# Layer norm and routing by block in the stages ahead of the experts of a six-layer network, experts on blocks 0 to 2 first, attention written out

## The reference

```python
x = x + 0.5 * ffn(ln(x))        # stage 0: silu(w1 x) * (w2 x), gelu, gelu, w3; 512 hidden
x = x + mixer(ln(x))            # stage 1: selective scan
x = x + 0.5 * ffn(ln(x))        # stage 2
x = x + 0.5 * moe(ln(x))        # stage 3
x = x + attention(ln(x))        # stage 4: 8 heads of 128, causal, k and v shared
x = x + 0.5 * moe(ln(x))        # stage 5

def _route(x, gate_w, gate_bias):
    scores = jax.nn.sigmoid(x @ gate_w.T)                       # 64 experts
    choice = scores + gate_bias
    group_scores = sum of the top 2 of each of 8 groups         # choice, 8 experts a group
    masked = where(group in the top 4, choice, 0)
    w = scores at the top 8 of masked
    return 2.5 * w / sum(w), zero elsewhere
# moe: sum over 64 experts (88 hidden) of rw[t, e] * silu(x Wg) * (x Wu) @ Wd, plus a shared one of 176
```

## Time and profile before

| What | us |
|---|---|
| Median of 3 runs (lowest, highest) | 1802.55 (1801.62, 1803.52) |
| Profiled execution | 1803.61 |
| Its span in the trace | 1801.8 |
| Start of stage 3 to the first weighted expert tile | 74.6 |
| Rest of stage 3 | 368.7 |
| Start of stage 4 to the first transposes | 29.2 |
| Rest of stage 4 | 232.8 |
| Start of stage 5 to the first weighted expert tile | 77.3 |
| Rest of stage 5 | 370.7 |

### The profile page before, as it was taken

How to read it: one execution, slowest core, us unless ns; L and a number is a source line. 1 busy time by engine, 2 the same in 40 slices (tenths; PEclk the granted TensorE clock), 3 DMA queues, 4 the chain that set the end, 5 groups by cost and what they waited for, 6 DMA issues and landing times.

```text
span 1801.8 us, 25450 instructions
## 1 busy us (share of the span) xinstructions
PE 1614.6 (90%) x6820; PEld 1208.8 (67%) x6820; DVE 1234.6 (69%) x2015; ACT 953.1 (53%) x1864; POOL 902.6 (50%) x786
## 2 busy tenths in 40 slices
PE   5999558877799985999999997999998599999998
PEld 3777323333367763788888885988885488888887
DVE  4555779999945645666666666877775466666666
ACT  3234565444434342565555564877773265655565
POOL 2000147766610023677777773344433277777776
PEclk9999779999989986999999999999997799999999
DMA  2000000000000001676777760000000366767765
GB/s 111 1 0 1 0 0 1 0 0 1 0 8 1 0 35 37 143 154 144 157 147 149 151 138 1 2 0 0 0 1 9 76 152 145 155 146 154 149 149 119
DMA packets 30035, 118.72 MB, mean 66 GB/s; under 512 B 5323, under 2 KB 17059, under 8 KB 18211
## 3 DMA queue, kind: packets, MB, share of 16 engines
q1 hardware_dynamic: 29987, 118.15, 29.8%
HBM read 116.03 MB, written 2.10 MB: 66 GB/s over the span
## 4 chain that ended last, share of the span: by engine, by line
PE 65%; DVE 3%; issue 2%; POOL 2%; ACT 2%; DMA 1%; POOLq 0%; DVEq 0%; SPq 0%; ACTq 0%
PE ps L218 18%; PE ps L220 18%; PE ps L219 18%; PE ps L1270 2%; PE ps L1255 1%; PE ps L1257 1%; PE ps L1256 1%; POOL m_hc L831 1%; PE ps L621 1%; DMA rwb<-rw_rows 1%; PE ps L240 1%; POOL e_lo L226 1%; PE ps L253 1%; PE ps L1258 1%; DMA rw_rows<-rwt 0%
## 5 line engine op out<-in xcount | busy, mean ns | idle before, releaser
L226 POOL TENSOR_TENSOR e_lo<-e_h,e_hi 128x512 fp32r<-128x512 f32 (+1 forms) x368 | 479.0, 1302 | 258.3 <-ACT e_hi L223 251.2
L1138 DVE TENSOR_TENSOR ps<-e_s,ps 128x512 f32<-128x512 f32 x352 | 245.0, 696 | 237.8 <-PE ps L220 179.1
L963 ACT ACTIVATE e_s<-ps 128x512 f32<-128x512 f32 (+1 forms) x368 | 220.2, 598 | 323.6 <-PE ps L220 323.5
L218 PE MATMUL ps<-xn_hi,eh 128*128 128x512 f32 x704 | 280.4, 398 | 22.8 <-DVE ps L1138 22.8
L219 PE MATMUL ps<-xn_lo,eh 128*128 128x512 f32 x704 | 279.1, 396 | 0.0
L220 PE MATMUL ps<-xn_hi,el 128*128 128x512 f32 x704 | 278.1, 395 | 0.0
L1149 DVE TENSOR_TENSOR e_h<-ps,rwb 128x512 f32<-128x512 f32 x352 | 243.3, 691 | 44.9 <-DMA rwb<-rw_rows 21.3
L223 ACT ACTIVATE e_hi<-e_h 128x512 fp32r<-128x512 f32 (+1 forms) x368 | 229.0, 622 | 48.8 <-DVE e_h L1149 25.7
L831 POOL TENSOR_TENSOR m_hc<-m_h,m_c 128x512 f32<-128x512 f32 x128 | 172.8, 1350 | 126.6 <-DVE m_h L787 124.3
L226 POOL TENSOR_TENSOR xn_lo<-ln_c,xn_hi 128x512 fp32r<-128x512 f32 (+1 forms) x24 | 34.2, 1427 | 327.9 <-ACT xn_hi L223 327.8
L621 PE MATMUL ps<-m_hc,const 128*128 128x512 f32 x256 | 149.3, 666 | 48.7 <-POOL m_hc L831 43.7
(11 more groups left out here) (238 smaller groups left out, 3192.5 us busy)
## 6 DMA issues: line engine op xcount, KB each, us to landing
rwb<-rw_rows SPq DMA_DIRECT2D x32, 704.0 KB
rwb<-rw_rows SPq DMA_DIRECT2D x40, 512.0 KB
e_raw<-in_experts SPq DMA_DIRECT2D x88, 192.0 KB, 5.5
rwb<-rw_rows SPq DMA_DIRECT2D x16, 640.0 KB
rwb<-rw_rows SPq DMA_DIRECT2D x24, 384.0 KB
rwb<-rw_rows SPq DMA_DIRECT2D x16, 448.0 KB
rwb<-rw_rows SPq DMA_DIRECT2D x16, 320.0 KB
rwb<-rw_rows SPq DMA_DIRECT2D x40, 128.0 KB
```

The lines of the kernel that those rows point to most:

```text
L218: pe.matmul(out, w_hi, x_hi, start=start, stop=False, skip_group_check=True)
L226: return eng.tensor_tensor(lo, full, hi.bitcast(F32), ALU.subtract)
L963: act.activation(e_s[0:rows_, buf, :], ps[0:rows_, 4, :], ACT.Silu).then_inc(S["silu"], 1)
L1138: dve.tensor_tensor(ps[0:rows_, 6 + buf % 2, :], e_s[0:rows_, buf, :], ps[0:rows_, 5, :], ALU.mult).then_inc(S["gated"], 1)
```

## The change

The routing is written per block of four token tiles (25 steps on 128 x 256 values) and moved:

- Stage 2 does logits, scores and LN for its blocks i-1 as before, and the routing steps of block 0 and 1 in its blocks 2 and 3. Stage 4 does the same for stage 5 (`spare_bank_fill`, `spare_bank_read`, bank 5), with the LN of stage 5 too.
- In stages 3 and 5, what is left (LN of block 3, routing of blocks 2 and 3) goes between the 8 shared tiles, which take blocks 0 to 2 first. Row weights of the first two chunks come by block (`moe_first_rows`, `rw_first{b}`).
- The last pair of stage 3 takes the tiles in another order (LAST_TILES), so that blocks 0 and 1 finish early and stage 4's LN of these two can be done there; stage 4 does blocks 2 and 3 at its start.
- The weights of the second chunk of a pair are split at tile 6 of the pair before (gate, up) and tile 1 (down), in place of tiles 0 and 3. `ah` and `al` are made in 8 slices of 288 columns in pair 20. The load of `a_raw` at the start of stage 3 stays, and one more stands behind the rows of chunk 8.
- The hardware loops of ffn and attention are written out in Python. `unused`, the buffer for table loads, has 40 columns, not 24. Buffers lie elsewhere.

```diff
+        def route_scores(act, R, b, bank):
+            act.wait_ge(*R("logits", b + 1))
+            if b >= 2:
+                act.wait_ge(*R("route", ROUTE_STEPS * (b - 1)))
+            act.activation(r_s[:, b % 2, :, :].rearrange("p t e -> p (t e)"), ps[:, bank, 0:4 * E], ACT.Sigmoid).then_inc(R["scores"], 1)
...
+        def route_turn(pe, R, b, bank):
+
+            pe.wait_ge(*R("route", ROUTE_STEPS * (b + 1)))
+            for t in range(4):
+                last = pe.transpose(ps[0:E, bank, t * P:(t + 1) * P], r_t[:, t * E:(t + 1) * E], ident)
+            last.then_inc(R["rw_t"], 1)
+
+        def route_rows(act, R, b, bank):
+            act.wait_ge(*R("rw_t", b + 1))
+            act.activation(rwt[:, cut(b)], ps[0:E, bank, :], ACT.Identity).then_inc(R["rwt"], 1)
...
+                        if R and i and layer_ == 1 and k == 2:
+                            route_logits(pe, R, N, i - 1, 0)
...
+                            if R and i:
+                                pe.wait_ge(*R("scores", i))
...
+                if R and i >= 2:
+                    route_turn(pe, R, i - 2, 4)
...
+                if R and i:
+                    route_scores(act, R, i - 1, 0)
+                if R and i >= 2:
+                    route_rows(act, R, i - 2, 4)
...
+                    if R and i >= 2 and layer_ == 1:
+                        route_pairs(dve, R, i - 2)
+                        route_groups(dve, R, i - 2)
+                        route_mask(dve, R, i - 2)
+                    if R and i >= 2 and layer_ == 2:
+                        route_top(dve, R, i - 2)
+                        route_weights(dve, R, i - 2)
...
+        SHARED_TILES = ((0, 0), (0, 1), (0, 2), (1, 0), (1, 1), (1, 2), (0, 3), (1, 3))
+        PAIR_TILES = tuple((j // NB, j % NB) for j in range(PER))
+        LAST_TILES = ((0, 0), (0, 1), (1, 0), (1, 1), (0, 2), (1, 2), (0, 3), (1, 3))
...
+                    if j == 1 and not (isinstance(i, int) and i == 0):
+                        down_high(i, 1, in_pair(i, 0))
...
+                    if j == 6 and not last:
+                        gate_up_high(i + 1, 1, in_pair(i, 8))
...
+                    if N and isinstance(i, int) and i == PAIRS - 2:
+                        part = slice(j * (NA // PER), (j + 1) * (NA // PER))
+                        if j == 0:
+                            act.wait_ge(a_in, 16)
+                        split_hi(act, ah[:, part], a_raw[:, part]).then_inc(a_hi, 1)
...
+            one_centre(dve, L, LAST, LAST)
+            route_pairs(dve, S, 2)
+            one_diagonal(dve, L, LAST)
+            route_groups(dve, S, 2)
+            shared_gate(0)
+            route_mask(dve, S, 2)
+            one_normalise(dve, L, LAST, LAST)
+            shared_gate(1)
+            shared_gate(2)
+            route_top(dve, S, 2)
+            shared_gate(3)
+            route_weights(dve, S, 2)
+            shared_gate(4)
+            route_pairs(dve, S, LAST)
+            shared_gate(5)
+            route_groups(dve, S, LAST)
+            shared_gate(6)
+            route_mask(dve, S, LAST)
+            shared_gate(7)
+            route_top(dve, S, LAST)
+            first_tile(0)
+            route_weights(dve, S, LAST)
...
+        def moe_first_rows(sp, S, b):
             rw_rows = d["rw_rows"][0 if S is E1 else 1]
+            sp.wait_ge(*S("rwt", b + 1))
+            sp.dma_start(rw_rows[:, cut(b)], rwt[:, cut(b)]).then_inc(S[f"rw_out{b}"], 16)
+            sp.wait_ge(*S(f"rw_out{b}", 16))
+            for ch in range(2):
+                for lo, hi, e in expert_rows(ch):
+                    sp.dma_start(rwb[lo:hi, ch, cut(b)], rw_rows[e:e + 1, cut(b)].broadcast_to([hi - lo, T])).then_inc(S[f"rw_first{b}"], 16)
...
+            moe_first_rows(sp, S, 2)
+            weights(2)
+            weights(3)
+            moe_first_rows(sp, S, 3)
...
+                if S is E1 and ch == 8:
+                    sp.dma_start(a_raw[:, :], d["attn"]).then_inc(a_in, 16)
...
+            def spare_bank_read(i, h):
+
+                if i and h == 1:
+                    pe.wait_ge(*N("centred", i))
+                if i and h == 3:
+                    pe.wait_ge(*N("dev", i))
+                if i and h == 5:
+                    pe.wait_ge(*N("normed", i))
+                if i >= 2 and h == 6:
+                    pe.wait_ge(*R("rwt", i - 1))
+                if i and h == 7:
+                    pe.wait_ge(*R("scores", i))
+
+            def spare_bank_fill(i, h):
+
+                if i and h == 0:
+                    pe.wait_ge(*A("x_new", i))
+                    pe.wait_ge(*A("q32", 8 * i + 3))
+                    one_mean(pe, N, i - 1, 5)
+                if i and h == 2:
+                    pe.wait_ge(*A("q32", 8 * i + 5))
+                    one_var(pe, N, i - 1, 5)
+                if i and h == 4:
+                    pe.wait_ge(*A("q32", 8 * i + 7))
+                    one_spread(pe, N, i - 1, 5)
+                if i >= 2 and h == 5:
+                    pe.wait_ge(*A("q32", 8 * i + 8))
+                    route_turn(pe, R, i - 2, 5)
+                if i and h == 6:
+                    if i + 1 < NB:
+                        pe.wait_ge(*A("k32", i + 2))
+                    route_logits(pe, R, N, i - 1, 5)
+
             def heads(i, last):
-                blk, following = bass.ds(i * T, T), bass.ds((i + 1) * T, T)
                 for h in range(HEADS):
                     if h:
                         score(i, h)
...
+                    if i >= 2 and h == 6:
+                        route_rows(act, R, i - 2, 5)
+                    if i and h == 7:
+                        route_scores(act, R, i - 1, 5)
...
+                    if i == 0 and h < 2:
+                        one_high(act, L, 2 + h)
...
+                    if i and h == 0:
+                        one_centre(dve, N, i - 1, 5)
+                    if i and h == 3:
+                        one_diagonal(dve, N, i - 1)
+                    if i and h == 4:
+                        one_normalise(dve, N, i - 1, 5)
+                    if i >= 2 and h == 0:
+                        route_pairs(dve, R, i - 2)
+                    if i >= 2 and h == 1:
+                        route_groups(dve, R, i - 2)
+                    if i >= 2 and h == 2:
+                        route_mask(dve, R, i - 2)
+                    if i >= 2 and h == 3:
+                        route_top(dve, R, i - 2)
+                    if i >= 2 and h == 4:
+                        route_weights(dve, R, i - 2)
```

More of the change, by code:

```diff
@@ L478, in ffn_pe, with ffn_act, block_ @@
                 pe.wait_ge(w_split, 4)
-            ffn_blocks(pe, block_)
-        def ffn_act(act, S, N):
-            def block_(i, blk, before, following):
+            for i in range(NB):
+                block_(i)
+        def ffn_act(act, S, N, R):
+            def block_(i):
+                if R and i == 1:
+                    moe_act(act, R)
                 for o in range(HC):
@@ L926, in moe_pe @@
-            for j in range(1, AHEAD):
-                expert_gate_up(0, j)
-            with pe.Fori(0, PAIRS - 1) as i:
+                    pe.wait_ge(*S("wd_lo", 2 * i + c + 1))
+                down(in_pair(i, j), eh[:, c, 0, :], el[:, c, 0, :], b, j % 4, False, tiles is LAST_TILES and c == 1, P)
+            one_mean(pe, L, LAST, LAST)
+            if S is E1:
+                pe.wait_ge(*S("small_lo", 2))
+            shared_gate_up(0)
+            one_var(pe, L, LAST, LAST)
+            shared_gate_up(1)
@@ L937, in moe_act @@
+            if N:
+                one_spread(pe, N, 1, 1)
         def moe_act(act, S):
@@ L940, in moe_act, with moe_act_tiles @@
             act.activation(sd_h[:, :, :], sd_raw[:, :, :], ACT.Identity).then_inc(S["small_hi"], 1)
-        def moe_act_tiles(act, S, attention):
-            load_table(act, ACT.Sigmoid)
-            for half in range(2):
-                act.wait_ge(*S("logits", half + 1))
-                act.activation(r_s[:, 8 * half:8 * half + 8, :].rearrange("p t e -> p (t e)"), ps[:, half, :], ACT.Sigmoid)\
-                    .then_inc(S["scores"], 1)
+        def moe_act_tiles(act, S, L, N):
             def gate_up_high(i, c, read):
@@ L1055, in shared_gate @@
                 dve.sem_inc(S["weighted"], 1)
-            steps = [0]
-            def step(ins):
-                steps[0] += 1
-                ins.then_inc(S["route"], 1)
-                if steps[0] % 3 == 1 and steps[0] // 3 < SHARED:
-                    shared_gate(steps[0] // 3)
-                dve.wait_ge(*S("route", steps[0]))
-            NGT = NTT * NG
-            small = [r_small[:, k, :] for k in range(4)]
-            def pairs_of(tile, lo, n):
-                v = tile[:, lo:lo + NGT * n].rearrange("p (g k) -> p g k", k=n)
-                return v[:, :, 0:n // 2], v[:, :, n // 2:n]
@@ new lines, in moe_dve @@
+            route_groups(dve, S, LAST)
[5 more added lines that the diff above has]
+            route_weights(dve, S, LAST)
```

(18 more changed lines are left out.)

718 lines of the change are left out of this document (394 added, 324 removed).

## The result

The changed kernel takes 1853.57 us (median of 4 runs, 1841.3 to 1856.43) against 1802.26 before: ratio 1.0266, 95% interval 1.0245 to 1.0287, so 2.7% slower. The profiled execution took 1853.06, its span is 1851.2, 49.4 us more than before.

A forecast was written before the change was run, and what follows sets the result against it. TensorE was taken to bound the expert loops and attention heads, with loose time at stage starts. Terms -34 - 37 + 12 + 11.5 - 8.5 + 45.7 = -10.3 gave span 1791.5, median 1792 us, range 1768 to 1813.

The forecast's parts named there:

- Attention heads, +45.7: Stage 4's heads: added logits, layer norm, routing and waits in blocks 1 to 3 cost 45.7 us, bounds 12 and 60.
- 0.8 slack for each, so 11.2 - 4.0 = 7.2 exposed: Attention blocks 2 and 3: five routing parts with norm steps, 11.2 us, of which VectorE's idle hides all but 7.2.
- The loop's term: Attention: writing out the loop drops register instructions between blocks, 0.8 x 3 = 2.4 us less.
- Expert loops, +11.5: Expert loops of stages 3 and 5: second attention-weight load, earlier wanted chunks and split slices cost 11.5 us.
- the weights of odd chunks are wanted two tiles earlier: 1 x 2: Expert loops: needing odd chunks' weights two tiles sooner costs 1 us in each of two loops.
- rival D: Expert loops: weights issued behind row weights land too late, 0.5 us in each of 42 chunks, +20, 1812 us; chance 0.14.
- Stage 3 start, -34: Start of stage 3: time to expert tile 4 falls from 80.9 to about 46.5 us, 34 us saved.
- Stage 5 start, -37: Start of stage 5: time to expert tile 4 falls from 83.6 to the same 46.5 us, 37 us saved.
- transposes and copy (1.1): Stage starts: transposing and copying block 3's row weights, on the way to tile 3, takes 1.1 us.
- Stage 2, +12: Stage 2: three sets of logits, the Sigmoid wait and routing steps put in there cost 12 us.
- Stage 3 end and stage 4 start, -8.5: Layer norm of blocks 0 and 1 under stage 3's last tiles: end 4 us longer, start 29.2 to about 16.
- Rival C: Routing steps collide with GpSimd's o_lo or q_lo in attention and stage starts, 1.05 us each, +17, 1809 us; chance 0.14.

The follow-up runs named there:

- no_steps: The changed kernel without the 25 routing steps of blocks 0 and 1 in attention, stage 5 using old weights for them: 1820.01 us, 1.0091 of the kernel before.
- later: The changed kernel with the five routing parts in attention blocks 2 and 3 moved behind the next head's normalise and q: 1851.16 us, 1.0247 of before.
- only_stage3: The changed kernel keeping routing in stage 2, stage 3's new start, written-out loops, early odd-chunk weights; no second attention-weight load, old plan for stages 4 and 5: 1792.33 us.
- odd_first: The changed kernel with each odd chunk's weights issued right behind the even chunk's, ahead of the even chunk's row weights: 1822.55 us, 1.0117 of before.
- ln_later: The changed kernel with attention's layer norm of blocks 0 and 1 at stage 4's start, not under stage 3's last tiles: 1849.41 us, 1.0281 of before.
- no_switch: The changed kernel with Exp for the Sigmoid and Identity for the square root in attention, so no table switches in the heads: 1840.58 us, 1.0212 of before.

## Why the prediction was wrong

The forecast was -10.3 us in the span; measured is +49.4. The terms add up to 60 us too little: the attention heads 19.9, the expert loops 14.0, the two stage starts 13.9, stage 3's end with stage 4's start 10.3, stages 0 and 1 3.1, and stage 2 1.9 the other way.

- *Attention heads, +45.7*: +65.6. The step that failed is the price of the routing steps, "0.8 slack for each, so 11.2 - 4.0 = 7.2 exposed". No such slack showed in head 0 (1.9 us more for a part of 1.9), and the steps pushed other things: by no_steps they cost 14 us a block, where their own time less the slack makes some 5. In the changed kernel four slow normalises a block (1.0 to 1.1 us each, where 2.1 us stood for collisions) and the lower clock (some 4 us a block, an estimate, where nothing stood) go with them. How the 14 us divide among these isn't shown, since in the run later the collisions only changed place. Block 1's term, 9.1, was right (10.2). Blocks 2 and 3 have 26.5 and 24.2, where 19.9 and 19.1 less 2.4 for the loop stood. The loop's term had the wrong sign: written out, the heads of only_stage3 took 1.6 us more, not 2.4 less. Block 0's 4.6 had no term.
- *Expert loops, +11.5*: 25.5 in the pairs. The step that failed is "the weights of odd chunks are wanted two tiles earlier: 1 x 2". They were late in nearly all pairs, as rival D had it; odd_first shows that it is their place in the queue. Rival D put it at 0.5 us in each chunk; it was 0.4 on average. The term for the second load, 5.5, was 8.
- *Stage 3 start, -34*: -27.2. *Stage 5 start, -37*: -29.9. Tile 4 came at 54.6 us in stage 3 and 53.3 in stage 5, not 46.5. Tile 0's gate was right (34, measured 35.3), and so were the write and the six reads (2.24 and 4.7 us, where 2.5 to 4.2 and 4.6 stood). The step that failed is "transposes and copy (1.1)", which left out that the transposes stand behind other products in TensorE's program, 5.9 and 4.4 us.
- *Stage 2, +12*: 10.1, right. In only_stage3 the same code took 168.3 us, 15.3 more than before, at a clock of 0.95 where the changed kernel had 0.99.
- *Stage 3 end and stage 4 start, -8.5*: +1.8, and 4.3 of block 0's 4.6 as well, where the layer norm of blocks 2 and 3 had gone (in only_stage3 block 0 takes 58.9 us again). The forecast priced the longer end at 4 us, and it was 11.5; the start shrank by 9.7 and not 13. ln_later and only_stage3 show that this part gains nothing.
- Rival C named the collision, and put it on the routing steps. In the heads of the changed kernel it fell on the normalise; in each of the two starts five routing steps took 0.9 to 1.3 us. The rule that spoke against the change, that of the Trainium skill (SBUF — State Buffer, "Who interferes with whom"), says of tensor_scalar that it can take the shared port pair by its fast mode; the row of 1.90 against 0.81 us agrees with that.
- The drain that the Trainium skill gives for each table switch (ScalarE: Activation LUTs, "What ACT_TABLE_LOAD costs") isn't borne out: no_switch would have had to be 20 us faster and was 10. The loads in the heads start 0.02 us after the instruction ahead of them ends.

The rivals were weighed as if only one of them would hold. What D and in part C describe came together, and the shortfalls of the starts and of stage 3's end, which were no rival at all, made another 24 us. Left open: why stages 0 and 1 took 3.1 us more in the changed profile (their code for TensorE is the same, and only_stage3 has 0.3 more; the granted clock of 220 to 300 us was 0.79 in the changed kernel, 0.83 before and 0.85 in only_stage3).

## What to carry to other kernels

Work moved from an idle start into a stage whose bound engine is 96 to 99% busy must be priced with what else it pushes in that stage: here 8.8 us of routing steps cost 14, and the rest of a block's added work 10 to 13. A product that another engine waits for is as late as its place in TensorE's program. When a consumer is moved earlier, move its load in the issuing queue too, and only that load: one line of order was worth 27 us (with most of the second load's 8 in them), and moving the weights of all chunks up cost 59. Undo the parts of a mixed change one by one; one of this one's, stage 2's routing for stage 3's start, was a gain of 17 us that the total hid.

## What the runs showed of the hardware

In a stretch at the full clock TensorE worked at half of it for some 6 us after an idle of 2.64 us (mean 0.68 over the head). After an idle of 3.04 us at head 7 the clock fell in block 1 (0.90) and not in block 2, and after idles of 1.7 to 1.8 us it fell in heads 4 and 6 of block 2 (0.85 and 0.86) and not in heads 0 and 5. With the idle filled by products nobody needs, the mean clock of heads 1 to 4 stayed at 1.00, it fell in other heads, and the kernel was no slower for 17 us of work. A normalise by VectorE, with one tensor input, took 1.0 to 1.1 us longer when it started between 0.03 us before and 0.3 us after the start of a GpSimd split (1.57 for 0.49 us over 512 columns, 1.42 for 0.42 over 384). A transfer of 192 KB landed 7.0 us after its issue in the median behind the broadcast reads of row weights, and 2.4 us after it when issued ahead of them.
